# Token lists made for four experts at a time, with 128 by 128 products, instead of for two with 64 by 64

## What is computed

```python
logits = xn @ router_weight.T + router_bias
probs = softmax(logits, axis=-1)
_, idx = top_k(logits.T, 512)          # each of 16 experts: its 512 best tokens
h = gelu(xn[idx] @ fc1 + b1);  y = h @ fc2 + b2
gates = take_along_axis(probs.T, idx, axis=1)
output = zeros.at[idx].add(y * gates)  # and divided by the sum of a token's gates
```

## Time and profile before

| | us |
|---|---|
| median of 3 runs (3893.57 to 3893.85) | 3893.75 |
| the profiled execution | 3893.05 |
| its span, first to last instruction | 3891.3 |
| TensorE busy in the span | 3630.7 (93%) |
| VectorE busy | 2260.8 (58%) |
| ScalarE busy | 1488.4 (38%) |
| TensorE's mean granted clock | 0.956 of full |
| first one-hot (L1334) to the experts' first instruction | 2327.4 to 2394.3 |

### The profile page before, as it was taken

The page is one execution under the profiler, slowest core; times in us unless marked ns, Lnnn a source line. Parts: engine busy times, 40 slices in busy tenths (PEclk is TensorE's granted clock), DMA queues, the critical chain, the costliest instruction groups (busy, mean ns, idle before and its releaser), DMA issues. The chain is left out here.

```text
span 3891.3 us, 55460 instructions
## 1 busy us (share of the span) xinstructions
PE 3630.7 (93%) x19935; PEld 2505.5 (64%) x19935; DVE 2260.8 (58%) x4972; ACT 1488.4 (38%) x2793; POOL 666.7 (17%) x859
## 2 busy tenths in 40 slices
PE   4899999999999999999999737999999999999995
PEld 3555556556555555565555337888888888888884
DVE  2576665675765766657657475444444444544456
ACT  1253443443444434434434322333333333333335
POOL 2022121121121221211211201011111111111113
PEclk8999999999999999999999855999999999999997
DMA  5234234233323252332332203343343343444448
GB/s 169 61 93 127 76 92 123 62 97 112 102 72 113 79 142 64 101 110 71 89 115 66 72 0 99 100 139 117 112 131 111 120 124 111 130 121 117 143 157 308
DMA packets 207200, 423.14 MB, mean 109 GB/s; under 512 B 45840, under 2 KB 48912, under 8 KB 198800
## 3 DMA queue, kind: packets, MB, share of 16 engines
q1 hardware_dynamic: 180304, 367.47, 30.6%
q0 software_dynamic: 14400, 35.14, 4.6%
q10 hardware_dynamic: 12288, 17.83, 1.7%
HBM read 246.23 MB, written 72.38 MB: 82 GB/s over the span
## 5 line engine op out<-in xcount | busy, mean ns | idle before, releaser
L833 ACT ACTIVATE probs<-scores_t 128x512 f32<-128x512 f32 (+3 forms) x1536 | 656.8, 496 | 574.6 <-PE scores_t L700 516.9
L1801 PE MATMUL m_ps_h<-m_tokens_t,m_w_parts 128*128 128x512 f32 x3072 | 739.7, 391 | 1.6 <-DVE m_tokens_t L1683 1.6
L1801 PE MATMUL m_ps_y<-m_w_parts,m_hidden_parts 128*128 128x512 f32 x3072 | 737.3, 390 | 0.6
L1801 PEld LDWEIGHTS m_ps_y<-m_w_parts,m_hidden_parts 128*128 128x128 f32 x3072 | 575.3, 188 | 125.8 <-issue 6.3
L1801 PEld LDWEIGHTS m_ps_h<-m_tokens_t,m_w_parts 128*128 128x128 f32 x3072 | 575.3, 188 | 120.1 <-issue 2.0
L889 DVE CUSTOM_DVE_ANT_0 shared_banks<-shared_banks,mask_q_rows 128x128 f32<-128x128 f32 (+3 forms) x1024 | 477.7, 515 | 176.4 <-PE shared_banks L657 173.9
L657 PE MATMUL shared_banks<-k_operands,q_operands 96*128 96x512 f32 (+3 forms) x1536 | 509.3, 379 | 23.7 <-DVE natural L880 8.9
L700 PE MATMUL scores_t<-q_operands,k_operands 128*128 128x512 f32 (+3 forms) x1536 | 494.7, 372 | 33.3 <-ACT probs L833 26.1
L1619 ACT ACTIVATE m_hidden<-m_ps_h,m_b 128x512 f32<-128x512 f32 x256 | 176.6, 690 | 791.1 <-PE m_ps_h L1801 777.9
L562 POOL TENSOR_SCALAR_AFFINE_SELECT probs<-probs 128x256 f32<-128x256 f32 x512 | 220.3, 433 | 1341.3 <-ACT probs L833 1340.7
L657 PEld LDWEIGHTS shared_banks<-k_operands,q_operands 96*128 96x128 f32 x1536 | 279.0, 191 | 263.7 <-issue 122.9
(11 more groups left out here) (243 smaller groups left out, 3225.2 us busy)
## 6 DMA issues: line engine op xcount, KB each, us to landing
m_w_raw<-in_w1T SPq DMA_DIRECT2D x64, 1024.0 KB, 5.2
m_w_raw<-in_w2T SPq DMA_DIRECT2D x64, 1024.0 KB, 7.5
wqk_group<-scratch_wqk SPq DMA_DIRECT2D x32, 1024.0 KB, 5.6
q_operands<-natural SPq DMA_DIRECT2D x192, 128.0 KB, 2.6
k_operands<-natural SPq DMA_DIRECT2D x192, 128.0 KB, 2.7
q_operands<-natural SPq DMA_DIRECT2D x384, 64.0 KB, 2.0
k_operands<-natural SPq DMA_DIRECT2D x384, 64.0 KB, 2.0
natural<-in_xT SPq DMA_DIRECT2D x8, 2048.0 KB, 9.8
```

What stands on the lines that cost most here:

```text
L833: act.activation(probs[:, slot_of(k, h // 2), h % 2, c0:HALF], st[:, (HG * k + h) % SCORE_BANKS, c0:HALF], ACT.Exp, scale=SCALE).then_inc( ...
L1801: mm = pe.matmul(bank, a, b, start=(first and n == 0), stop=(final and n == len(pairs) - 1))
```

## The change

The rounds make four experts' lists (`SET` = 4, `SETS` = 4 rounds). Weights and moving operand of each product now have 128 columns (4 experts x 2 kinds x 16 rows, and 4 experts x 32), 64 products a round. `join` becomes 128 by 64. ScalarE copies four blocks a round. The parts of the gates are made two at a time after the one-hots of rounds 0 and 1, and their DMA stands on SyncE's queue ahead of the lists'.

```diff
+    SET = 4
...
-        oh_row = sb("s_row_onehot", [P, 2, 2, HI_N, NCH], BF16)
-        oh_tok = sb("s_row_tokens", [P, 2, 2, 2, HI_N, NCH], BF16)
-        oh_col = sb("s_col_onehot", [P, 2, 2, LO_N, NCH], BF16)
-        join = sb("s_join", [2 * PAIR, PAIR])
+        oh_row = sb("s_row_onehot", [P, 2, SET, HI_N, NCH], BF16)
+        oh_tok = sb("s_row_tokens", [P, 2, SET, 2, HI_N, NCH], BF16)
+        oh_col = sb("s_col_onehot", [P, 2, SET, LO_N, NCH], BF16)
+        join = sb("s_join", [SET * PAIR, SET * HI_N])
...
-            for it in range(PAIRS):
+            sp.wait_ge(gates_ready, 1)
+            sp.dma_start(table.rearrange("(c p) k -> p c k", p=P)[:, :, D:TABLE], gated[:]).then_inc(probs_out, 16)
+            for it in range(SETS):
                 sp.wait_ge(list_ready, it + 1)
-                sp.dma_start(list_dram[2 * it:2 * it + 2, :].rearrange("a (h l) -> (a h) l", l=LO_N), lists[:, it % 2, :]
+                sp.dma_start(list_dram[SET * it:SET * it + SET, :].rearrange("a (h l) -> (a h) l", l=LO_N), lists[:, it % 2, :]
                              ).then_inc(list_out[it % 2], 16)
-                if it == GATES_AT:
-                    sp.wait_ge(gates_ready, 1)
-                    sp.dma_start(table.rearrange("(c p) k -> p c k", p=P)[:, :, D:TABLE], gated[:]).then_inc(probs_out, 16)
...
-                for r in range(2):
+                for r in range(SET):
                     rows = slice(r * PAIR, (r + 1) * PAIR)
                     act.activation(parts[rows, it % 2], ps_list[rows, it % 2, r * LO_N:(r + 1) * LO_N], ACT.Copy
                                    ).then_inc(list_copied, 1)
...
-                pe.wait_ge(row_pids, 2 * it + 2)
-                pe.wait_ge(onehots, 2 * it + 2)
+                pe.wait_ge(row_pids, SET * it + SET)
+                pe.wait_ge(onehots, SET * it + SET)
                 for n in range(NCH):
-                    mm = pe.matmul(ps_list[:, b, 0:2 * LO_N], oh_tok[:, b, :, :, :, n].rearrange("p r a h -> p (r a h)"),
+                    mm = pe.matmul(ps_list[:, b, 0:SET * LO_N], oh_tok[:, b, :, :, :, n].rearrange("p r a h -> p (r a h)"),
                                    oh_col[:, b, :, :, n].rearrange("p r l -> p (r l)"),
...
-                if 1 <= it <= 4:
-                    dve.wait_ge(d, step[0])
-                    gate(it - 1)
+                if it < 2:
+                    for n in (2 * it, 2 * it + 1):
+                        dve.wait_ge(d, step[0])
+                        gate(n)
                 if it > 1:
                     write_list(it - 2)
```

More of the change, by code:

```diff
@@ L1020, in build_selection @@
         gsum = sb("s_gate_sums", [P, 3, NCH])
-        oh_row = sb("s_row_onehot", [P, 2, 2, HI_N, NCH], BF16)
-        oh_tok = sb("s_row_tokens", [P, 2, 2, 2, HI_N, NCH], BF16)
-        oh_col = sb("s_col_onehot", [P, 2, 2, LO_N, NCH], BF16)
-        join = sb("s_join", [2 * PAIR, PAIR])
-        parts = sb("s_list_parts", [2 * PAIR, 2, LO_N])
-        lists = sb("s_list", [PAIR, 2, LO_N], U32)
+        oh_row = sb("s_row_onehot", [P, 2, SET, HI_N, NCH], BF16)
+        oh_tok = sb("s_row_tokens", [P, 2, SET, 2, HI_N, NCH], BF16)
+        oh_col = sb("s_col_onehot", [P, 2, SET, LO_N, NCH], BF16)
+        join = sb("s_join", [SET * PAIR, SET * HI_N])
+        parts = sb("s_list_parts", [SET * PAIR, 2, LO_N])
+        lists = sb("s_list", [SET * HI_N, 2, LO_N], U32)
         ps_lg = ps("s_ps_lg", [P, TT, ROWS])
@@ L1029, in build_selection @@
         ps_cnt = ps("s_ps_cnt", [ROWS, 16])
-        ps_join = ps("s_ps_join", [PAIR, HALF])
-        ps_list = ps("s_ps_list", [2 * PAIR, 2, HALF])
+        ps_join = ps("s_ps_join", [SET * HI_N, HALF])
+        ps_list = ps("s_ps_list", [SET * PAIR, 2, HALF])
         zeroed, cand_ready, signed = sem("s_zeroed"), sem("s_cand_ready"), sem("s_signed")
@@ L1043, in build_selection @@
         block = ctx.enter_context(nc.Block())
-        PAIRS = E_N // 2
+        SETS = E_N // SET
         BITS = 31
         SEARCHES = 1 + (BITS - 1) // 2
-        GATES_AT = 5
-        join_bank = (ps_pos[0:PAIR, 0, 0:LO_N], ps_join[:, 0:LO_N])
+        join_bank = (ps_pos[0:SET * HI_N, 0, 0:LO_N], ps_join[:, 0:LO_N])
         def shift_of(i):
@@ L1058, in _ @@
             sp.dma_start(x[:], logits_dram.rearrange("e (s t) -> (e s) t", t=T)).then_inc(x_in, 16)
-            for it in range(PAIRS):
+            sp.wait_ge(gates_ready, 1)
+            sp.dma_start(table.rearrange("(c p) k -> p c k", p=P)[:, :, D:TABLE], gated[:]).then_inc(probs_out, 16)
+            for it in range(SETS):
                 sp.wait_ge(list_ready, it + 1)
-                sp.dma_start(list_dram[2 * it:2 * it + 2, :].rearrange("a (h l) -> (a h) l", l=LO_N), lists[:, it % 2, :]
+                sp.dma_start(list_dram[SET * it:SET * it + SET, :].rearrange("a (h l) -> (a h) l", l=LO_N), lists[:, it % 2, :]
                              ).then_inc(list_out[it % 2], 16)
-                if it == GATES_AT:
-                    sp.wait_ge(gates_ready, 1)
-                    sp.dma_start(table.rearrange("(c p) k -> p c k", p=P)[:, :, D:TABLE], gated[:]).then_inc(probs_out, 16)
             sp.wait_ge(probs_out, 16)
             for r in range(2):
-                sp.wait_ge(list_out[r], 16 * PAIRS // 2)
+                sp.wait_ge(list_out[r], 16 * SETS // 2)
         @block.gpsimd
@@ L1096, in _ @@
             pool.memset(join[:], 0.0).then_inc(join_zero, 1)
-            for n, (r, value) in enumerate(((0, 1.0), (0, float(P)), (1, 1.0), (1, float(P)))):
+            for n, (r, value) in enumerate((r, value) for r in range(SET) for value in (1.0, float(P))):
                 cols = join[:, r * HI_N:(r + 1) * HI_N]
@@ L1121, in copy_list @@
                                    ).then_inc(list_copied, 1)
-            for it in range(PAIRS):
-                for r in range(2):
-                    act.wait_ge(rows_ready, 2 * it + 1 + r)
+            for it in range(SETS):
+                for r in range(SET):
+                    act.wait_ge(rows_ready, SET * it + 1 + r)
                     if it >= 2:
@@ L1131, in _ @@
                     copy_list(it - 1)
-            copy_list(PAIRS - 1)
+            copy_list(SETS - 1)
         @block.tensor
@@ L1171, in _ @@
             mm.then_inc(pos_turned, 1)
-            pe.wait_ge(join_zero, 5)
+            pe.wait_ge(join_zero, 2 * SET + 1)
             def join_list(it):
@@ L1177, in join_list @@
                     pe.wait_ge(list_ready, it - 1)
-                pe.wait_ge(list_copied, 2 * it + 2)
+                pe.wait_ge(list_copied, SET * it + SET)
                 pe.matmul(join_bank[it % 2], join[:], parts[:, it % 2, :], start=True, stop=True).then_inc(joined, 1)
-            for it in range(PAIRS):
+            for it in range(SETS):
                 b = it % 2
                 if it >= 2:
-                    pe.wait_ge(list_copied, 2 * it - 2)
-                pe.wait_ge(row_pids, 2 * it + 2)
-                pe.wait_ge(onehots, 2 * it + 2)
+                    pe.wait_ge(list_copied, SET * it - SET)
+                pe.wait_ge(row_pids, SET * it + SET)
+                pe.wait_ge(onehots, SET * it + SET)
                 for n in range(NCH):
-                    mm = pe.matmul(ps_list[:, b, 0:2 * LO_N], oh_tok[:, b, :, :, :, n].rearrange("p r a h -> p (r a h)"),
+                    mm = pe.matmul(ps_list[:, b, 0:SET * LO_N], oh_tok[:, b, :, :, :, n].rearrange("p r a h -> p (r a h)"),
                                    oh_col[:, b, :, :, n].rearrange("p r l -> p (r l)"),
@@ L1193, in _ @@
                     join_list(it - 1)
-            join_list(PAIRS - 1)
+            join_list(SETS - 1)
         @block.vector
@@ L1331, in _ @@
                     dve.wait_ge(list_mm, it - 1)
-                for r in range(2):
-                    e = 2 * it + r
+                for r in range(SET):
+                    e = SET * it + r
                     dve.tensor_tensor(oh_row[:, b, r], row[:, e:e + 1, :].to_broadcast([P, HI_N, NCH]),
                                       iota[:, 0:HI_N, :], ALU.is_equal).then_inc(rows_ready, 1)
-                for r in range(2):
-                    e = 2 * it + r
+                for r in range(SET):
+                    e = SET * it + r
                     dve.tensor_tensor(oh_col[:, b, r], col[:, e:e + 1, :].to_broadcast([P, LO_N, NCH]),
                                       iota[:], ALU.is_equal)
-                dve.wait_ge(rows_ready, 2 * it + 2)
-                for r in range(2):
+                dve.wait_ge(rows_ready, SET * it + SET)
+                for r in range(SET):
                     dve.tensor_tensor(oh_tok[:, b, r, 1], oh_row[:, b, r], cid[:].unsqueeze(1).to_broadcast([P, HI_N, NCH]),
                                       ALU.mult).then_inc(onehots, 1)
-                if 1 <= it <= 4:
-                    dve.wait_ge(d, step[0])
-                    gate(it - 1)
+                if it < 2:
+                    for n in (2 * it, 2 * it + 1):
```

(6 more changed lines are left out.)

## The result

The changed kernel takes 3938.51 us (median of 4 runs, 3937.69 to 3938.87) against 3893.66 before: ratio 1.0118, 95% interval 1.0102 to 1.0134. It was to be 3896.7, within 3880 to 3899.

What follows compares the result with a forecast made beforehand. TensorE's chain of list products was taken as the bound; lead 4.7, products -0.8, joins -1.5, rounding 0.1 and tail 0.5 sum to +3.0 us, hence 3896.7 us, range 3880 to 3899.

Steps and rivals of the forecast that it cites:

- What bounds the lists: List building in the selection stage: TensorE's chain of products bounds it, busy 59.18 of 59.20 us at 1.2 GHz.
- The lead: Before the first list product: one-hots of four experts instead of two delay TensorE's start, a loss of 4.69 us.
- A product of full width: List chain: 128 by 128 takes 0.217 us, load and stream overlapping; 256 replace 512 at 0.110, gaining 0.8 us.
- rival A: List products: the clock rises to 2.4 GHz; 3880.6 us if held (0.15), 3887.4 if it falls back (0.05); chance 0.20.
- the joins: Between list chains: six at 0.42 us become two at 0.53, a gain of 1.5 us.
- the tail: After the last list chain: four block copies instead of two and a wider join, a loss of 0.5 us.
- Gates: Selection stage, first two sets: their work stays hidden under products, barely (cover 1.3 us); their DMA's early start is worth nothing.
- Nothing else: Rest of the kernel: no other effect on the time; VectorE's four saved casts of 0.18 us are hidden.
- moved later as a block: Experts after the lists: first products only shift in time, running 2.7 us at low clock; 1.3 us less or more.
- B: List products: a fixed price of 0.110 us each whatever the width, VectorE then the bound; 3880.6 us, chance 0.07.
- C: List products: the weight load gets cheaper at full width, so the stream alone counts, 0.198 us; 3891.9 us, chance 0.06.
- D: List products: load and stream no longer overlap, 0.42 us each; 3949 us, deciding from 0.236 us on; chance 0.05.

Runs made afterwards that it cites:

- shift64: after_pad24 with the column one-hots (the moving operand) placed 64 bytes further in their partition: 3894.59 us, ratio 1.0006 to the kernel before the change.
- early_gates: Kernel before the change, with only the gates' parts made in the first two rounds and their DMA ahead of the lists': 3892.69 us, ratio 1.0002.
- after_pad24: Changed kernel with 24 more TensorE instructions (already satisfied waits) right ahead of the experts' loop: 3903.31 us, ratio 1.0031 to the kernel before the change.
- before_pad232: Kernel before the change, with 232 more TensorE instructions (satisfied waits) spread over the search's idle time: 3930.81 us, ratio 1.0099.
- the probe: after_pad24 with 640 extra products ahead of the last chain, in ten groups of differing widths, read in steps or contiguously: 3990.27 us.

## Why the prediction was wrong, point by point

- *What bounds the lists*: right. TensorE stood between the chains only for its joins.
- *The lead*: +4.69 forecast, +4.68 measured (9.60 from first one-hot to first product, 4.92 before).
- *A product of full width*: 0.217 forecast, 0.253 measured, 256 x 0.036 = +9.2 us. The step took load and stream to overlap freely because they do in the f32 transpose. That transpose reads contiguous columns; here both sides step over the same 16 bytes of each 128. shift64 gives 0.217. That the transpose's 0.221 lies so near is partly luck: it is f32 and contiguous, and a contiguous bf16 stream of that width takes 0.107. Nor is the load's part of 0.110 a number of ticks (132), since L1205 took it at both clocks; what rival A's products in steps would take at 2.4 GHz no run shows. The mis-sized term explains the list part: 3.0 + 9.2 = 12.2 of 12.2, with the joins 0.2 better than forecast (0.43 each) and the tail 0.3 worse.
- *Gates*: hidden in after, and their early DMA worth nothing, as forecast. In early_gates, with its shorter first chain, 0.7 us of them shows.
- *"Nothing else", and the experts "moved later as a block"*: the step that failed most, 38.1 us of 45.8. It counted what instructions do and left out that a shorter program moves the code behind it. Of the 38.1, 36.3 lie in the six later distances (they sum to 1106.1 us, 6 x 178.3 = 1069.8) and 1.6 in the first, 0.64 of it the first stop; early_gates has 1.3 there without any stop, so the rest of it can be noise. Idle time makes 25.0 us, and most of the rest goes with products at the low clock behind the stops. after_pad24 takes it away and before_pad232 makes it without the change.
- *Rival A*: the clock stayed at 0.50 in all the list products of after. In the probe it rose only once the stream was contiguous. *B* would have had 0.110. *C* was half right: the load of 128 is cheaper, but even without the clash (shift64) the stream alone takes 0.217, not 0.198. *D* named the point from which the products decide, 0.236 us, and they passed it, but not by its mechanism: load and stream do overlap (L1203).
- *The range* held no case for a cost outside the stage, so it could not hold the result.

Left open: why load and stream clash in the probe's 64 by 64 group and not in chains of that shape, and at which place exactly the loop begins to be fetched anew. The runs show moves by 0 and +60 places without it, by +130 and -24 with it, which fits a loop that may touch seven blocks and not eight, but no run looked at the border.

## What to carry to other kernels

When instructions are removed ahead of a long hardware loop, count by how many, modulo 256, and look at the instruction queue's packets and at idle time put down to "issue" in the loop; 24 filler instructions in an idle spot gave back 35 us here. Before widening a product, look at the step with which its operands are read: two neighbouring columns in 16 bytes nearly halved its price here (0.110 to 0.060), at no cost to the writer as long as it wrote runs of four. And where load and stream both read in steps of 128 bytes, put them on different 16-byte lines of the 128; 64 bytes apart is what was tried.

## What the runs showed of the hardware that was not expected

- A loop of 1669 instructions on TensorE costs nothing or 6.1 us a turn, by its place alone; at another place it is fetched anew in each turn for under 1 us.
- Load and stream of a 128 by 128 product slow each other by 36 ns where both step by 128 bytes on the same 16-byte line, and not at all with 64 bytes between them. With 64 weights it was 11 to 19 ns in the probe and nothing in the chains of before.
- A load of 128 bf16 weights in steps of 128 bytes is no slower than one of 64 (within 0.107 and 0.110 us), and that of 64 took the same at either clock.
- VectorE writes runs of four bf16 elements at full pace and single ones in steps eight times as slowly (1.21 and 9.46 us for 2048).
